# Attention divides its values by their sums in place, by quarters of a chunk; the router's stage loads finished values

## The reference

```python
scores = jnp.einsum('bhqd,bhkd->bhqk', q, k) / jnp.sqrt(jnp.float32(HD))
scores = jnp.where(causal, scores, -jnp.inf)
attn = jax.nn.softmax(scores, axis=-1)
y = jnp.einsum('bhqk,bhkd->bhqd', attn, v)
y = y.transpose(0, 2, 1, 3).reshape(b, s, d)
return y @ w_o
...
logits = xf.astype(jnp.float32) @ w_router.astype(jnp.float32)
probs = jax.nn.softmax(logits, axis=-1)
```

## Time and profile before

| | us |
|---|---|
| median of 3 runs | 2514.23 (2504.64 to 2518.49) |
| the profiled execution | 2516.99 |
| its span, first to last instruction | 2515.0 |
| busy: PE / DVE / ACT / POOL | 2121.5 / 1494.1 / 1091.7 / 532.5 |

### The profile page before, as it was taken

One profiled execution on the slowest core, in us unless ns is written; L12 is line 12 of the kernel. 1 busy time (PEld: TensorE's weight loads), 2 busy tenths in 40 slices (PEclk: granted clock), 3 DMA queues, 4 the chain that ended last, 5 costly groups with the idle time before them and its releaser, 6 DMA issues. The chain is left out here.

```text
span 2515.0 us, 42690 instructions
## 1 busy us (share of the span) xinstructions
PE 2121.5 (84%) x18144; PEld 1244.3 (49%) x18144; DVE 1494.1 (59%) x2300; ACT 1091.7 (43%) x1070; POOL 532.5 (21%) x445
## 2 busy tenths in 40 slices
PE   6799999999978699799999999974830699999990
PEld 3444444444433344344444444431530688888880
DVE  7768888888858765476666666602452344434323
ACT  5678888888842222124444444450200233322210
POOL 0000000000001122324555555562204000000005
PEclk9899999999989899689999999997855799999995
DMA  6312112112122135530220400006103533333307
GB/s 251 134 42 71 47 60 71 53 55 71 54 86 109 59 142 202 132 80 22 52 51 18 97 22 20 8 20 165 50 0 125 184 109 113 109 113 113 110 26 271
DMA packets 85773, 221.30 MB, mean 88 GB/s; under 512 B 10320, under 2 KB 11472, under 8 KB 78768
## 3 DMA queue, kind: packets, MB, share of 16 engines
q1 hardware_dynamic: 74496, 176.50, 21.9%
q0 software_dynamic: 11088, 42.08, 4.7%
HBM read 154.72 MB, written 59.51 MB: 85 GB/s over the span
## 5 line engine op out<-in xcount | busy, mean ns | idle before, releaser
L449 ACT ACTIVATE m_step<-m_ub,gat_bias 128x2048 bf16<-128x2048 f32 x256 | 493.8, 1992 | 119.9 <-DVE m_mask L526 106.0
L1149 DVE TENSOR_REDUCE t_rm<-t_m 128x1 f32<-128x512 f32 (+3 forms) x640 | 375.5, 608 | 207.2 <-PE t_m L1198 129.8
L1109 ACT ACTIVATE t_E<-t_s 128x1024 f32<-128x1024 f32 (+3 forms) x320 | 277.6, 894 | 377.1 <-PE t_s L1218 184.0
L526 DVE TENSOR_TENSOR m_mask<-m_step,gat_adjT 128x2048 bf16<-128x2048 bf16 x256 | 306.8, 1222 | 83.7 <-ACT m_step L449 73.4
L1088 POOL TENSOR_TENSOR t_total<-t_E 128x1024 f32<-128x1024 f32 (+2 forms) x160 | 307.8, 1935 | 173.4 <-PE t_d L1242 173.4
L1198 PE MATMUL t_m<-t_K,t_Q 96*128 96x512 f32 (+3 forms) x640 | 275.6, 453 | 33.5 <-DVE t_rm L1149 17.1
L1198 PEld LDWEIGHTS t_m<-t_K,t_Q 96*128 96x128 f32 x640 | 125.7, 200 | 187.6 <-DVE t_rm L1149 126.3
L566 PE MATMUL m_bd<-m_mask,m_S 128*32 128x512 bf16 x3072 | 211.3, 379 | 8.0 <-DVE m_mask L526 7.7
L566 PE MATMUL m_bd<-gat_adjT,m_S 128*32 128x512 bf16 x3072 | 211.3, 379 | 4.9 <-PE m_dn L566 4.9
L566 PE MATMUL m_bd<-m_mask,m_neg 128*32 128x512 bf16 x3072 | 211.2, 379 | 0.0
L1215 PE MATMUL t_s<-t_Q,t_K 97*128 97x512 f32 (+3 forms) x640 | 209.2, 403 | 0.5 <-ACT t_E L1109 0.5
(11 more groups left out here) (270 smaller groups left out, 3290.8 us busy)
## 6 DMA issues: line engine op xcount, KB each, us to landing
a_adj<-in_adj SPq DMA_DIRECT2D x16, 1024.0 KB, 4.9
m_ub<-scratch_uac SPq DMA_DIRECT2D x16, 1024.0 KB, 4.7
e_w1r<-in_L_ffn_w SPq DMA_DIRECT2D x8, 2048.0 KB, 8.2
e_w2r<-in_L_ffn_w SPq DMA_DIRECT2D x8, 2048.0 KB, 8.8
t_Q<-scratch_parts SPq DMA_DIRECT2D x48, 256.0 KB, 4.7
scratch_xe<-o_zeros POOLq DMA_DIRECT2D x10, 1024.0 KB, 4.2
e_xe<-scratch_xe SPq DMA_DIRECT2D x8, 1280.0 KB, 9.2
scratch_ye<-e_ye POOLq DMA_DIRECT2D x40, 256.0 KB, 2.3
```

Of the source, the lines that this page charges most:

```text
L449: act.activation(step[n % RELUS][:, :], ub[h % 2][:, :], ACT.Relu, bias=bias[:, j, h:h + 1], scale=BIG).then_inc(step_ready, 1)
L526: dve.tensor_tensor(mask[n % MASKS][:, :], step[n % RELUS][:, :], adjT[:, j, :], ALU.min).then_inc(mask_ready, 1)
L1109: act.activation(E[n % 3][:, two, off:BANK], ps_s[:, two, off:BANK], ACT.Exp, scale=SCALE).then_inc(exp_done[z], 1)
L1149: dve.tensor_reduce(rm[:, h, t, ch:ch + 1], ps_m[i % 2][:, 0:w], AX, ALU.max).then_inc(entry_read, 1)
```

## The change

In attention the stores of the sums go. Four steps and more after a chunk's end, DVE divides: call r of `divide(u, r)` multiplies quarter r-1 (128 columns) of `out` by the inverted sums and inverts quarter r of `den`; five calls a chunk, one at the end of a step. SP stores a chunk once, in one DMA, when its four quarters are done, and some stores move behind other DMAs of the queue. ACT's next copy into the same `den` waits for the division instead of the store. The last chunk is divided behind the loop.

In the router the sums, their reciprocal, the round trip through DRAM and the four products go. The values come in four DMAs (one a chunk) of 128 partitions, `W` is loaded behind the first, PE waits for `W` and the chunk alone.

```diff
@@ attention, SP
                 def store(q, c):
                     u = q * NC + c
...
+                    sp.wait_ge(normed, 4 * (u + 1))
+                    sp.dma_start(o_dram[q * P:(q + 1) * P, c * BANK:(c + 1) * BANK], out[u % 2][:, :]).then_inc(o_sent[u % 2], 16)
...
                     if more:
                         load_q(q + 1, 0)
+                    if q:
+                        store(q - 1, 3)
+                    maxima(q, 2)
                     store(q, 0)
-                    maxima(q, 2)
                     if more:
                         load_q(q + 1, 1)
                     store(q, 1)
                     maxima(q, 3)
                     if more:
                         load_q(q + 1, 2)
+                        maxima(q + 1, 0)
                     store(q, 2)
                     if more:
-                        maxima(q + 1, 0)
                         maxima(q + 1, 1)
                         load_q(q + 1, 3)
                     if q + 2 < QUADS:
                         load_k(q + 2)
-                    store(q, 3)
+                store(QUADS - 1, 3)
@@ attention, ACT
                 if u >= 2:
-                    act.wait_ge(d_sent[u % 2], 64 * (u // 2))
+                    act.wait_ge(normed, 4 * (u - 1))
@@ attention, DVE
+                PARTS, WIDE = 4, BANK // 4
+
+                def divide(u, r):
+                    if r > 0:
+                        part = slice((r - 1) * WIDE, r * WIDE)
+                        dve.wait_ge(inverted, u * PARTS + r)
+                        if r == 1:
+                            dve.wait_ge(o_copied, u + 1)
+                        dve.tensor_tensor(out[u % 2][:, part], out[u % 2][:, part], den[u % 2][:, part],
+                                          ALU.mult).then_inc(normed, 1)
+                    if r < PARTS:
+                        part = slice(r * WIDE, (r + 1) * WIDE)
+                        if r == 0:
+                            dve.wait_ge(d_copied, u + 1)
+                        dve.reciprocal(den[u % 2][:, part], den[u % 2][:, part]).then_inc(inverted, 1)
...
                 for q in range(QUADS):
                     for s in range(NS):
+                        n = q * NS + s - 4
+                        if n >= 0 and n % NS in END.values():
+                            turn += [(n // NS * NC + STEPS[n % NS][0], r) for r in range(PARTS + 1)]
...
                         coming = next_until(q, s)
+                        if turn:
+                            divide(*turn.pop(0))
                     own, coming = coming, 0
                 copy(QUADS - 1, NC - 1)
+                for r in range(PARTS + 1):
+                    divide(QUADS * NC - 1, r)
@@ router, SP
+                load_o(0)
                 sp.dma_start(W[:, :, :], w_o.rearrange("(k p) n -> p k n", p=P)).then_inc(w_in, 16)
...
+                for c in range(1, NC):
+                    load_o(c)
@@ router, PE
-                pe.wait_ge(w_in, 48)
+                pe.wait_ge(w_in, 16)
                 for t in range(T):
                     if t % 4 == 0:
-                        pe.wait_ge(o_ready, t // 4 + 1)
+                        pe.wait_ge(o_in[t // 4], 16)
@@ router, DVE
-                dve.wait_ge(den_in, 16)
-                dve.reciprocal(share[:, :], share[:, :]).then_inc(share_ready, 1)
                 for t in range(T):
-                    if t % 4 == 0:
-                        c = t // 4
-                        dve.wait_ge(o_in[c], 16 * (P // DH))
-                        dve.wait_ge(by_in[c % 2], 16 * (P // DH) * (c // 2 + 1))
-                        part = oT[:, :, c * BANK:(c + 1) * BANK]
-                        dve.tensor_tensor(part, part, by[c % 2][:, :, :], ALU.mult).then_inc(o_ready, 1)
```

More of the change, by code:

```diff
@@ L985, in stage_attention @@
         o_sent = [sem(f"t_o_sent{i}") for i in range(2)]
-        d_sent = [sem(f"t_d_sent{i}") for i in range(2)]
+        inverted, normed = sem("t_inverted"), sem("t_normed")
         with nc.Block() as block:
@@ L1155, in entry @@
                         dve.sem_inc(m_ready, 1)
-                own, coming = START, 0
+                own, coming, turn = START, 0, []
                 for i in range(START):
@@ L1274, in _, with stage_router @@
                 denominators(QUADS * NS // 2 - 1)
[L1277 removed]
+def stage_router(nc, sem, keep, w_o, g2, w_router, o_dram, res_dram):
     X1, Z, mv, rstd, prob, ident = (keep[n] for n in ("X1", "Z", "mv", "rstd", "prob", "ident"))
@@ L1282, in stage_router @@
         oT = st.sb("oT", [P, KD, N])
-        share = st.sb("share", [P, H * N // P])
-        by = [st.sb(f"by{c}", [P, KD, BANK]) for c in range(2)]
         grow = st.sb("grow", [P, D])
@@ L1295, in stage_router @@
         o_in = [sem(f"r_o_in{c}") for c in range(NC)]
-        by_in = [sem(f"r_by_in{c}") for c in range(2)]
-        den_in, share_ready, share_out, o_ready = (sem("r_" + n) for n in ("den_in", "share", "share_out", "o_ready"))
+        g_in, wr_in = sem("r_g_in"), sem("r_wr_in")
         w_in, link, full, y_ready, ms_ready, ve_ready, sd_ready, z_ready, zT_full, zT_ready = (
@@ L1304, in _, with load_o @@
             def _(sp):
[L1306 to L1312, removed]
+                ov = o_dram.rearrange("(k p) n -> p k n", p=P)
+                def load_o(c):
+                    cut = slice(c * BANK, (c + 1) * BANK)
+                    sp.dma_start(oT[:, :, cut], ov[:, :, cut]).then_inc(o_in[c], 16)
+                load_o(0)
                 sp.dma_start(W[:, :, :], w_o.rearrange("(k p) n -> p k n", p=P)).then_inc(w_in, 16)
-                sp.dma_start(grow[:, :], g2.partition_broadcast(P)).then_inc(w_in, 16)
-                sp.dma_start(Wr[:, :, :], w_router.rearrange("(k p) n -> p k n", p=P)).then_inc(w_in, 16)
+                for c in range(1, NC):
+                    load_o(c)
+                sp.dma_start(grow[:, :], g2.partition_broadcast(P)).then_inc(g_in, 16)
+                sp.dma_start(Wr[:, :, :], w_router.rearrange("(k p) n -> p k n", p=P)).then_inc(wr_in, 16)
                 for c in range(4):
@@ L1323, in _ @@
             def _(pool):
[L1324 to L1333, removed]
                 for t in range(T):
@@ L1352, in logits @@
                     pe.wait_ge(zT_ready, t + 1)
+                    if t == 0:
+                        pe.wait_ge(wr_in, 16)
                     for k in range(KD):
@@ L1407, in _ @@
                 root_of_inverse(dve, lk, rms, sd, ve)
-                dve.wait_ge(w_in, 48)
+                dve.wait_ge(g_in, 16)
                 for t in range(T):
@@ L1857, in program @@
                 stage_router(nc, sem, keep, ins["L0_ffn_w_o"], ins["L0_ffn_g2"], ins["L0_ffn_w_router"],
-                             scratch["o"], scratch["rec"], scratch["res"])
+                             scratch["o"], scratch["res"])
                 stage_slots(nc, sem, keep, scratch["xe"])
@@ L1861, in program @@
             stage_combine(nc, sem, keep, scratch["res"], scratch["ye"], outs[0])
-SCRATCH = {"uac": ((3, H, N), F32), "near": ((H, N), F32), "parts": ((4, D, N), F32), "o": ((H * (DH + 1), N), F32), "rec": ((H, N), F32), "res": ((N, D), F32),
+SCRATCH = {"uac": ((3, H, N), F32), "near": ((H, N), F32), "parts": ((4, D, N), F32), "o": ((D, N), F32), "res": ((N, D), F32),
            "xe": ((EXPERTS * CAP, D), F32), "ye": ((EXPERTS * CAP, D), F32)}
```

6 lines of the change are left out of this document (2 added, 4 removed).

## The result

The changed kernel takes 2497.88 us (median of 10 executions, 2493.27 to 2501.71), the kernel before 2513.09 us beside it: a ratio of 0.9938, with a 95% interval of 0.9924 to 0.9952. It is 15 us faster, where 5 us slower had been forecast; the stated range began at 2498.0, 0.1 us above it. The profiled execution took 2497.15 us (span 2495.4), 19.8 us less than that of before.

The account below looks back on a forecast made before the run. PE nearly fills attention (620 of 653 us), DVE and PE handing over tiles; PE idles at the router's start. Attention +34, router -29: +5 us on 2514.23, so 2519; about one in ten beyond each end of 2498 to 2545.

Parts of the forecast that it names:

- +34 in attention: Attention: 25.6 us of late DVE work plus 8 us of clock falls lengthen it by 34 us, bounds 15 and 60.
- Clock: Attention: 18 new PE stalls of 0.9 to 1.4 us bring 5 falls to half speed, 8 us; bounds 0 and 18 falls.
- Lateness: Attention: division's products and reciprocals overrun DVE's gaps, products also wait for POOL; next reduces late by 25.6 us in all.
- the placement worked out in the prediction: Attention, odd step ending at 1314.34: product waits 0.83 us for POOL, so the next reduce starts 1.34 us late.
- the table: Attention: lateness of the next reduce, summed for 70 placements with entries beside them: 28.6 us, less 3 for overlap.
- All lateness passed on: Attention: PE has no slack, as an entry already waited for DVE, so all 25.6 us of DVE lateness delay PE.
- POOL first: Rival, step 12 of quads 1 to 3: product waits for both POOL additions, 4.7 us; +20, 2539 us; chance 0.24.
- no product above 2 us: Expected sign in the profile: no product lasts over 2 us; one above 4 would mean POOL started ahead of it.
- Join and router's start: Between attention and router: start 5.3 us later, PE begins 10 us after that, three 3.05 us waits go; gain 29 us.
- SP's queue: Attention: later stores on SP stay hidden with 11 us spare; otherwise a chunk would wait a few us, 15 times.
- nearly covered: Rival, attention: products slip between POOL's instructions, no clock falls; costs 15 to 18 us, 2502 us in total; chance 0.20.
- a case whose extra 8 us rested on the clock: The main forecast: attention +34 us including 8 us of clock falls, 2519 us in total, 2508 to 2530; chance 0.40.

Follow-up runs that it names:

- the experiment on even steps: The changed kernel with products only at the end of even steps (not step 12), up to two at once, reciprocals one a step: 2493.56 us, 0.9917 of before.

## Why the prediction was wrong, point by point

The forecast was +34 in attention and -29 in the router; the profiles show +13.7 and -31.6, and 1.7 less elsewhere, -19.6 in all. By medians it is -15. Two terms of the sum failed, both in attention: the clock, put at +8, and the size of the lateness, put at 25.6.

- **Clock, +8 forecast, about -2 measured.** This is the larger failure. The forecast took two stalls and their granted clocks in one execution and gave 5 of 18 new stalls of 0.9 to 1.4 us a fall each, on top of the falls of before. Of the new stalls over 0.5 us there were 11, ten of them 0.52 to 0.92, and the falls were no more than before. The pair of profiles had 3 fewer, about -5 us, and that was mostly chance: by their mean granted clocks the 29 executions of the kernel before spent 433 us at half clock and the 10 of the changed one 409; 41.0 and 20.5 of these belong to the router's start in the profiles, where PE stands for the most part. What is left is 3 us at half clock, one fall, as an estimate. With it the medians add up: 18.5 - 31.6 - 1.6 = -14.7, with -15.2 measured.
- **Lateness, 25.6 forecast, 17.6 measured net of the clock.** The mechanism was right: after even steps a product of 0.28 us, after odd ones one of 1.08 that ends with POOL's addition. The size was off. For the placement worked out in the prediction it was 1.05 us and not 1.34: the product ended 0.15 us behind POOL and not 0.29, and each of the two next instructions started 0.07 to 0.08 before its predecessor's end. I had taken 0.05 for a whole placement. For some 25 placements that the table has late by more than 0.3 us, 0.24 each makes 6 of the 8 us, as an estimate; how the rest divides, isn't shown. What product and reciprocal last (0.29 and 0.95 forecast, 0.28 and 0.94 measured) was right.
- **All lateness passed on.** Nearly right. PE waits 0.59 us ahead of an entry that didn't wait before. Against the kernel without division the reduce behind a product that waited out POOL in an odd step is 1.03 to 1.15 us later, and 0.85 to 1.1 of that stays; up to 0.2 is given back at once.
- **POOL first.** The rival's place was right, its price not. In step 12 the product started at 1299.34 and POOL at 1299.37, so it cost nothing. Where POOL was first (in the experiment on even steps) the product waited for the one instruction that ran, 2.4 us and not 4.7; the step from one whole instruction of POOL to both was the rival's own. The sign "no product above 2 us" failed once, with 2.48 us at 1664.05, in steps in which no entry waits.
- **Join and router's start, -29 forecast, -31.6 measured.** The first load came 8.3 us behind the last copy of the sums (8.7 forecast), the first product 8.0 behind that load (10 forecast, the rate), and the gaps at the borders of chunks are gone.
- **SP's queue.** Hidden, as forecast: in the changed kernel's attention PE has no wait for a DMA of the queries. The kernel without division can't show this, since its stores don't wait. A product two steps later did bring such a wait, 3.13 us.
- **The rivals.** The third case, "nearly covered", had named 15 to 18 us for attention, no falls, 2502 in all, and the numbers are near that (17.6 net, 2497.9, no more falls than before), though not by its mechanism: the products did not slip past POOL, they waited, but for less. That its number came out is in part luck. It was given 0.20, below a case whose extra 8 us rested on the clock.

## What to carry to other kernels

Work that is put on an engine with idle time is free only in gaps that are long enough where it stands; find the gap behind each instruction that another engine waits for, and place the pieces by it. Here the same 73 us of work cost 18 us or 1, by their steps and by one swap in SP's queue that the later steps had made necessary. Two SBUF inputs on DVE make POOL's schedule part of yours. And when two profiles are compared, take out first what the clock did: falls of 1.6 us each, up to seven in this stage, are larger than most terms of such a sum, and the change need not have caused them.

## What was not expected of the hardware

- The same stall of 1.3 us had a fall of the clock behind it in one execution (granted 0.59) and none in another (1.00); what decides isn't shown. Half clock for 3.4 us cost 1.6 us. With 14 stalls of 2.6 to 3.4 us one attention stage had 85 us at half clock.
- A DVE product held up by POOL waited for the one instruction of POOL that ran, also where the next followed without a gap (2.41 us beside 4.75 us of POOL). Whether that always holds is open: in the kernel before, a DVE tensor-with-scalar instruction of the router lasted 4.46 us, until four of POOL's were through, and 0.54 us where it wasn't held up.
- By the profile's records, DVE instructions that waited for nothing started 0.07 and 0.08 us before the one ahead ended, in the placement read above.
- Loads of 1 MB over 128 partitions landed at 340 GB/s for five and 260 for two, with the start included, and at some 400 between landings, against 236 GB/s where many smaller ones and POOL's broadcasts shared the engines.
